# Router logits from the turned x and the scanned states in four column strips

## What is computed

```python
# attention part: x is (2, 2048, 256)
decays = sigmoid(x @ Wd + bd);  inj = x @ Wi + bi
states = scan(h -> d * h + i)                      # along the 2048 tokens
attn = layernorm(states) * gamma + beta + x
x = layernorm(x + attn)                            # called y below
# routed feed-forward part, E = 8 experts, 4 chosen per token
gate = y @ Wg.T + routing_bias
weights = softmax over the 4 largest of gate
out = swiglu(y, shared) + sum_e weights_e * swiglu(y, expert_e)
x = layernorm(y + out)
```

## Time and profile before

| | |
|---|---|
| median of 3 runs | 996.76 us (995.49 to 996.99) |
| the profiled execution's own time | 993.37 us |
| its span | 991.6 us |
| PE busy | 972.4 us, 98% |
| DVE busy | 559.6 us, 56% |
| ACT busy | 508.9 us, 51% |
| POOL busy | 544.6 us, 55% |

### The profile page before, as it was taken

How to read it: one execution, slowest core, us unless ns; L and a number is a source line. 1 busy time by engine, 2 the same in 40 slices (tenths; PEclk the granted TensorE clock), 3 DMA queues, 4 the chain that set the end, 5 groups by cost and what they waited for, 6 DMA issues and landing times.

```text
span 991.6 us, 25401 instructions
## 1 busy us (share of the span) xinstructions
PE 972.4 (98%) x8054; PEld 799.8 (81%) x8054; DVE 559.6 (56%) x1411; ACT 508.9 (51%) x1250; POOL 544.6 (55%) x513
## 2 busy tenths in 40 slices
PE   9998999999999999999999999999999999999997
PEld 4665666788887888888788878788888887887886
DVE  4998687745544455545444545454455454544686
ACT  3676354455554555555444545445455554554366
POOL 4554027766733347623955016076888880885873
PEclk9999999999999999999999999999999999999999
DMA  6959024355542333353245214228764882795785
GB/s 229 248 139 184 1 55 131 94 161 146 166 114 78 104 92 97 98 173 95 61 144 145 49 48 128 54 50 190 127 98 75 127 124 53 109 131 87 101 146 144
DMA packets 168051, 113.86 MB, mean 115 GB/s; under 512 B 113596, under 2 KB 160191, under 8 KB 166848
## 3 DMA queue, kind: packets, MB, share of 16 engines
q0 software_dynamic: 29808, 58.37, 27.5%
q1 hardware_dynamic: 115888, 33.15, 16.4%
q10 hardware_dynamic: 22304, 21.76, 6.6%
HBM read 47.09 MB, written 43.12 MB: 91 GB/s over the span
## 4 chain that ended last, share of the span: by engine, by line
PE 83%; POOL 6%; DVE 4%; DMA 3%; issue 3%; ACT 1%; SPq 1%; POOLq 0%; ACTq 0%; DVEq 0%
PE psA L1072 51%; PE psB L1103 21%; PE psA L1020 5%; POOL y_sum L758 3%; DMA rows_by_place<-y_rows,place 2%; POOL rows_by_place L694 2%; PE psB L1106 1%; PE psC L1054 1%; PE psA L1103 1%; DMA y_sum<-rows_by_place,place 1%; PE psB L1033 1%; PE psC L1047 1%; PE psC L1174 0%; SPq L518 0%; DVE g_lo L1504 0%
## 5 line engine op out<-in xcount | busy, mean ns | idle before, releaser
L873 ACT ACTIVATE sil<-psA 128x256 f32<-128x256 f32 (+1 forms) x456 | 178.8, 399 | 283.6 <-PE psA L1072 259.1
L758 POOL DMA_INDIRECT y_sum<-rows_by_place,place x128 | 199.7, 1560 | 82.8 <-issue 38.0
L1494 DVE SCALAR_TENSOR_TENSOR g<-psA,sil 128x256 f32<-128x256 f32 (+1 forms) x160 | 72.0, 450 | 306.5 <-ACT sil L873 306.3
L1072 PE MATMUL psA<-xb_odd,work 128*128 128x256 f16 x1980 | 221.1, 273 | 0.5 <-issue 0.5
L1072 PEld LDWEIGHTS psA<-xb_odd,work 128*128 128x128 f16 x1980 | 193.2, 98 | 24.1 <-issue 1.5
L1103 PE MATMUL psB<-work,g_hi 128*128 128x256 f16 x1260 | 211.1, 273 | 0.0
L1072 PE MATMUL psA<-xb,work 128*128 128x256 f16 x1782 | 199.0, 273 | 2.2 <-issue 1.1
L1072 PEld LDWEIGHTS psA<-xb,work 128*128 128x128 f16 x1782 | 173.8, 98 | 23.9 <-issue 3.8
L1494 DVE SCALAR_TENSOR_TENSOR psC<-psA,sil 128x256 f32<-128x256 f32 (+3 forms) x296 | 133.1, 450 | 77.6 <-ACT sil L873 71.2
L1103 PE MATMUL psB<-work,g_lo 128*128 128x256 f16 x630 | 171.7, 273 | 0.0
L705 POOL DMA_INDIRECT rows_by_place<-y_rows,place x96 | 95.2, 992 | 135.1 <-DMA rows_by_place<-y_rows,place 121.3
(11 more groups left out here) (176 smaller groups left out, 1033.3 us busy)
## 6 DMA issues: line engine op xcount, KB each, us to landing
stage<-wpack POOLq DMA_DIRECT2D x9, 2176.0 KB, 8.9
rows_by_place<-eb ACTq DMA_DIRECT2D x57, 256.0 KB
work<-xT SPq DMA_DIRECT2D x7, 512.0 KB, 6.0
work<-half_beta SPq DMA_DIRECT2D x6, 512.0 KB, 4.8
work<-x_tok POOLq DMA_DIRECT2D x6, 512.0 KB, 6.5
rows_by_place<-eb ACTq DMA_DIRECT2D x6, 384.0 KB
rows_by_place<-zeros SPq DMA_DIRECT2D x1, 2112.0 KB, 13.2
rows_by_place<-y_rows,place POOLq DMA_INDIRECT x128, 2.5
```

The costliest lines, as they stand in the source:

```text
L758: pool.indirect_dma_start(out=y_sum[:, n, :], out_offset=None, in_=xs, in_offset=bass.IndirectOffsetOnAxis(ap=place[:, k, n:n + 1], axis=0 ...
L873: act.activation(sil[r0:r0 + n, c % SLOTS, 0:T], psA[0:n, chunk_bank(c, T), 0:T], ACT.Silu, scale=1.0 / (XS * WS)).then_inc(silu_ready, 1)
L1072: last = pe.matmul(dst, W[:, ws, k, ci, :], xb[slot][:, KD * xs_ + k, 0:T], start=(k == 0 and n == 0), stop=(k == KD - 1 and n == 2))
L1494: dve.scalar_tensor_tensor(gated_rows(g, c, 0, n, T), src, 1.0 / (XS * WS), sil[r0:r0 + n, c % SLOTS, 0:T], ALU.mult, ALU.mult).then_inc(g ...
```

## The change

The normalized row is y = rs2 * (rs1 * (state - mean) * gamma + x + beta/2 - mean2), where rs2 carries a factor two in the kernel's scaling, so the logits are linear in x and in the states up to the factors rs1 and rs2 of a token. The gate weights are centred once (their column means subtracted), both plain, for x, and multiplied by gamma and centred again, for the states. TensorE multiplies xt and st, which lie turned in SBUF already, with these weights: the weights are stationary, 32 columns wide (8 plus 8 of use, the rest zero), and each of the four token tiles of a step writes its own 32 partitions of PSUM (Q * j), in float32. ScalarE copies the sums and adds the part of beta as a bias, TensorE turns them with one transpose, ScalarE copies them once more, and POOL combines the two parts with rs1, rs2 and the routing bias in four operations.

- gone: y_turned, turned, gates, VectorE's logits, the BRIDGE matmuls, tile yT
- new at the start: weight_sums and beta_sum (TensorE), centre_first and centre_second (VectorE, ahead of the scans), two memsets of POOL, one small copy of ScalarE
- new per step: gate_sums, turn_parts, copy_sums, copy_parts, POOL's logits
- xT has three buffers, the one of yT being the third; a load waits for gate_sums of the step three before it, and the first fetch for the third load instead of the first
- psC is used by the new sums; rstd1 and first_norm wait for the logits of two steps before
- in step 6 the first up chunk stands ahead of gate_sums(7); chunks 1 and 2 follow the loop

```diff
+            def logits(s):
+                b, g0 = s % B, tok(s) // P
+                scaled, summed, normed_ = (gate_parts[:, n, :, :] for n in range(3))
+                pool.wait_ge(parts_ready, s + 1)
+                pool.wait_ge(rstd2_ready, s + 1)
+                g = gate_tally
+                g.add(pool.tensor_tensor(scaled, parts[:, b, :, E:2 * E],
+                                         rs1[b][:, :].unsqueeze(2).to_broadcast([P, JT, E]), ALU.mult))
+                g.wait()
+                g.add(pool.tensor_tensor(summed, scaled, parts[:, b, :, 0:E], ALU.add))
+                g.wait()
+                g.add(pool.tensor_tensor(normed_, summed, rs2[b][:, :].unsqueeze(2).to_broadcast([P, JT, E]),
+                                         ALU.mult))
+                g.wait()
+                pool.tensor_tensor(gate[:, g0:g0 + JT, :], normed_, rb.unsqueeze(1).to_broadcast([P, JT, E]),
+                                   ALU.add).then_inc(logits_ready, 1)
...
                 rstd2(s)
+                logits(s)
...
-            def turned(s):
-
-                act.wait_ge(yT_turned, s + 1)
-                act.activation(yT, psC[:, :, :], ACT.Copy).then_inc(yT_ready, 1)
+            def copy_sums(s):
+                act.wait_ge(parts_summed, s + 1)
+                if s:
+                    act.wait_ge(parts_turned, s)
+                act.activation(part_rows[:, :], psC[:, 0, P * (s % B):P * (s % B + 1)], ACT.Identity,
+                               bias=beta_part[:, 0:1]).then_inc(parts_copied, 1)
+            def copy_parts(s):
+                act.wait_ge(parts_turned, s + 1)
+                if s >= B:
+                    act.wait_ge(logits_ready, s - B + 1)
+                act.activation(parts[:, s % B, :, :],
+                               psC[:, 1, P * (s % B):P * (s % B + 1)]
+                               .rearrange("p (t q) -> p t q", q=Q)[:, :, 0:2 * E], ACT.Copy).then_inc(parts_ready, 1)
...
+            def weight_sums():
+                for n in range(2):
+                    if n:
+                        pe.wait_ge(centring_steps, KD + 1)
+                    for k in range(KD):
+                        rhs = centred[:, k * E:(k + 1) * E] if n else wg[:, k * E:(k + 1) * E]
+                        last = pe.matmul(psC[:, 1, 2 * P + n * E:2 * P + (n + 1) * E], ones32[:, :], rhs,
+                                         start=(k == 0), stop=(k == KD - 1))
+                    last.then_inc(sums_ready, 1)
...
+            def gate_sums(s):
+                b = s % B
+                if s >= B:
+                    pe.wait_ge(parts_copied, s - B + 1)
+                for n, src in enumerate((xt[s % XT], st[b])):
+                    if n:
+                        pe.wait_ge(states_ready, 2 * s + 2)
                     for k in range(KD):
+                        for j in range(JT):
+                            last = pe.matmul(psC[Q * j:Q * (j + 1), 0, P * b:P * (b + 1)],
+                                             turned_weights[:, n, k, :], src[:, k, j * P:(j + 1) * P],
+                                             start=(n == 0 and k == 0), stop=(n == 1 and k == KD - 1))
+                last.then_inc(parts_summed, 1)
...
             products(1, [0])
             pe.wait_ge(small_loaded, 16)
             pe.wait_ge(consts_ready, NCONST)
+            weight_sums()
+            beta_sum()
+            gate_sums(0)
             states(0)
             products(1, [1])
...
-                if s:
-                    y_turned(s - 1)
+                turn_parts(s)
...
-                if s >= EARLY:
-                    up(SH, 0, [s - EARLY], TL, early_slot(0))
-                if s:
-                    gates(s - 1)
+                    up(SH, 0, [0], TL, early_slot(0))
                 if s + 1 < NSTEP:
+                    gate_sums(s + 1)
                     states(s + 1)
-            y_turned(NSTEP - 1)
-            up(SH, 0, [2], TL, early_slot(0))
-            gates(NSTEP - 1)
+            up(SH, 0, [1, 2], TL, early_slot(0))
             up(SH, 0, [3, 4, 5], TL, early_slot(0))
...
+            centre_first()
+            centre_second()
             for s, m in ((0, 0), (0, 1), (1, 0)):
                 scan(s, m)
```

More of the change, by code:

```diff
@@ L194, in build @@
         eb = sb("eb", [P, JL, D], F32)
+        ones32, part_rows = (eb[:, 0, n * P:(n + 1) * P] for n in range(2))
+        parts = eb[:, 1, 0:B * JT * 2 * E].rearrange("p (b t e) -> p b t e", b=B, t=JT)
+        gate_parts = eb[:, 2, 0:3 * JT * E].rearrange("p (n t e) -> p n t e", n=3, t=JT)
+        centred = eb[:, 2, 3 * JT * E:(3 * JT + KD) * E]
         row_weights = ([sb(f"row_weights{n}", [P, JB, E], F32) for n in range(2)]
@@ L209, in build @@
         passed = sem("passed")
-        xT_loaded = [sem(f"xT_loaded{b}") for b in range(B)]
+        xT_loaded = [sem(f"xT_loaded{b}") for b in range(B + 1)]
         x_loaded = [sem(f"x_loaded{b}") for b in range(B)]
@@ L846, in shared_high @@
                     .then_inc(shared_high_ready, 1)
-            for s in range(AHEAD):
-                acts(s)
+            acts(0)
+            acts(1)
+            act.wait_ge(beta_summed, 1)
+            act.activation(beta_part[:, 0:1], psC[:, 1, 3 * P:3 * P + 1], ACT.Copy).then_inc(beta_part_ready, 1)
+            act.wait_ge(beta_part_ready, 1)
+            copy_sums(0)
             for s in steps:
@@ L1045, in y_turned, with beta_sum @@
+            def beta_sum():
+                pe.wait_ge(turned_weights_ready, 1)
                 for k in range(KD):
                     for j in range(JT):
[L1047 to L1052, removed]
-                    for k in range(KD):
-                        last = pe.matmul(psC[:, 0, j * E:(j + 1) * E], yT[:, k, j * P:(j + 1) * P],
-                                         wg[:, k * E:(k + 1) * E], start=(k == 0), stop=(k == KD - 1))
-                last.then_inc(logits_summed, 1)
+                        last = pe.matmul(psC[Q * j:Q * (j + 1), 1, 3 * P:3 * P + 1], turned_weights[:, 0, k, :],
+                                         half_beta_cols[:, k:k + 1], start=(k == 0), stop=(k == KD - 1))
+                last.then_inc(beta_summed, 1)
@@ L1325, in shared_low, with centre_first, centre_second @@
                         dve.tensor_copy(lo[r:end, full:m], hi[r:end, full:m]).then_inc(shared_low_ready, 1)
-            def logits(s):
-                g0 = tok(s) // P
-                dve.wait_ge(logits_summed, s + 1)
-                dve.tensor_tensor(gate[:, g0:g0 + JT, :], psC[:, 0, 0:JT * E].rearrange("p (t e) -> p t e", e=E),
-                                  rb.unsqueeze(1).to_broadcast([P, JT, E]), ALU.add).then_inc(logits_ready, 1)
+            def centre_first():
+                dve.wait_ge(sums_ready, 1)
+                for k in range(KD):
+                    c.add(dve.scalar_tensor_tensor(turned_weights[:, 0, k, 0:E], psC[:, 1, 2 * P:2 * P + E], -1.0 / D,
+                                                   wg[:, k * E:(k + 1) * E], ALU.mult, ALU.add))
+                c.wait()
+                for k in range(KD):
+                    ins = dve.tensor_scalar(centred[:, k * E:(k + 1) * E], turned_weights[:, 0, k, 0:E],
+                                            gamma_cols[:, k:k + 1], None, ALU.mult)
+                c.add(ins)
+            def centre_second():
+                dve.wait_ge(sums_ready, 2)
+                c.wait()
+                dve.tensor_single_scalar(half_beta_cols[:, :], beta_cols, 0.5, ALU.mult)
+                for k in range(KD):
+                    ins = dve.scalar_tensor_tensor(turned_weights[:, 1, k, E:2 * E], psC[:, 1, 2 * P + E:2 * P + 2 * E],
+                                                   -1.0 / D, centred[:, k * E:(k + 1) * E], ALU.mult, ALU.add)
+                ins.then_inc(turned_weights_ready, 1)
+            c = Tally(dve, centring_steps)
             ngroup, turns, nblock, upto, b_upto, start, limit, tail = (cnt[:, n, :] for n in range(8))
@@ L1585, in _ @@
             ffn_block(0, TL, beside=routed_beside(0))
-            logits(NSTEP - 1)
             t.wait()
```

72 lines of the change are left out of this document (44 added, 28 removed).

## The result

The median is 1000.68 us (998.91 to 1001.95, 5 runs) against 995.49 (994.08 to 996.99, 5 runs) for the kernel before beside it: 1.0055 times, 95% interval 1.0041 to 1.0068, so slower, by about half a per cent. The profiled execution of after took 1001.72 us, its span is 1000.0.

The account below looks back on a forecast made before the run. TensorE, busy 98%, was taken as the bound, so only the opening before it resumes at 116.81 us could matter. Terms of +7.05, +0.2, +1.1 and -3.9 gave +4.45 on the 996.76 median: 1001.2 us, own range 999 to 1004, stated 995.5 to 1009.5.

Parts of the forecast that it names:

- The start: Opening, up to T(1): VectorE's scans queue behind the centring, first scan at 18.55 instead of 9.99; +7.05 us, the largest term.
- T(1): End of step 1's second moments on VectorE; forecast at 41.8 us instead of 34.73.
- The strips: TensorE's gate_sums per step: four strips writing disjoint partitions should overlap, 1.3 us taken, between 0.85 and 3.4.
- G: Time of TensorE's gate_sums matmuls per step, taken as 1.3 us; the sum hardly reacts up to 2.2.
- The loop: T(1) to T(6): POOL's added logits delay rstd1's power, which holds VectorE's scan; 51.95 against 51.77, +0.2 us.
- The last step: T(6) to T(7): logits(6) stands ahead of rstd1(7) and the second fetch; 8.85 instead of 7.73, +1.1 us.
- Behind the loop: From X to TensorE's resumption behind routing: third and fourth chunks run during chosen_early; -3.9 us (3.6 to 4.2).
- X: T(7), the end of step 7's second moments on VectorE; 94.23 us before, 102.6 predicted.
- The sum: All terms at TensorE's resumption behind the routing decision: 7.05 + 0.2 + 1.1 - 3.9 = +4.45 us, 121.3 instead of 116.81.
- Rivals 1: Loop: POOL never holds VectorE's scan, so -4.2 instead of +0.2; total +0.05, 996.8 us; chance 0.18.
- 3 (VectorE alone): VectorE alone sets the pace everywhere behind step 1; total -4.8, 992 us; chance 0.10.
- Rival 2: TensorE's strips run one after another, its step taking 11.3 us; total +12, 1008.8 us; chance 0.17.

Follow-up runs that it names:

- the scans first: Changed kernel with VectorE's scans of step 0 each put ahead of one half of the centring; 0.9999 times the kernel before.
- the kernel with fillers: Changed kernel plus matmuls of zeros with unread results in TensorE's idle stretches (7, 28 and 24); 1.0056 times the kernel before.
- one strip: Changed kernel plus 16 more matmuls like gate_sums per step from step 1, all into one strip of 32 partitions, result unread; 1.0237 times the kernel before.
- both edits: Changed kernel with scans ahead of centring and POOL's logits(s - 1) ahead of rstd2(s); 0.9935 and, in another set, 0.9966 times the kernel before.
- the logits late: Changed kernel with POOL's logits(s - 1) moved ahead of rstd2(s), after rstd1(s) and add_x(s + 1); 0.9992 times the kernel before.

## Why the prediction came out as it did

- **The start** (+7.05 at T(1), measured +8.80). Right in place and cause: with the scans first 4.6 of it go. Its size was short by 1.75. The scan came 0.36 later than 18.55; the rest, 1.4, is TensorE's clock, which the prediction thought about only behind the loop, and which the kernel with fillers gives back (1.38). TensorE waits 0.84, 0.40 and 1.59 us within the four microseconds of the centring; then the second half of gate_sums takes 1.08 and states(0) 1.97 instead of 1.04. The weight fetch was issued at 26.70, as forecast (27), and cost nothing.
- **The strips** (G 1.3 between 0.85 and 3.4). Measured 1.01, by the control against one strip 3.4. The lower end was nearer, for the reason given: nothing orders one strip behind another. By the Trainium skill (TensorE: Matmul & The Clock Gate, Part 3, Packing small matmuls), G would be an estimated 1.4 from three strips of 512 columns; four strips of 128 columns in float32 do better here.
- **The loop** (+0.2, measured +1.30: 53.07 against 51.77). The right pair of engines and nearly the right price, but the wrong one waits. The prediction had the scan wait 0.95 for POOL's power. In fact the scan is first by 0.07 and POOL's rstd1 is held behind it, and then the product with rs1 waits 1.18 (0.90 in the steps with low_rows) instead of 0.95 and 0.77. Three times 0.23 and twice 0.13 are 0.95 of the 1.1 us that were missing. The Trainium skill (SBUF — State Buffer, on the shared port pair) has the rule that whichever starts first holds it for the whole instruction: the 1.19 at 59.52 agrees, and the rule cuts both ways. POOL's four operations took 0.24 and 0.25 each, 1.3 with their gaps, not 1.1.
- **The last step** (8.85, measured 9.05). Right, against 7.73 before: rstd1(7) comes late behind logits(6) and the second fetch, and the product waits 1.60 instead of 0.24. With both edits it is gone (7.74); the 8.85 with the logits late alone is TensorE's clock.
- **Behind the loop** (-3.9, measured -4.13). The cause named, the third chunk at X + 0.5 instead of X + 5.0, fits: with the chunk held back again 3.7 are gone, though part of that is the clock. The lower clock of the chunks (5.76 for the two instead of 4.06) costs nothing at the resumption; the prediction paid 0.3. The limit that is left is ScalarE's normed(7) ahead of the third silu, which the prediction had in its sum (third gated at X + 6.7, measured X + 6.05).
- **The sum.** At the resumption it gave +4.45, measured +7.29: 2.8 short (start 1.75, loop 1.1, last step 0.2, less 0.2 in the tail). The time of 1000.68 nevertheless meets the 1001.2, and that is partly luck. The forecast stood on the 996.76 of three runs, while before ran at 995.49 beside the changed kernel, so as a difference +4.45 was forecast and +5.19 measured. Of the +7.29 at the resumption only 5.19 are seen in the medians: the two spans differ by 8.4, but before's profiled execution lies 2.1 below the median beside it and after's 1.0 above. The prediction's lift of 3.4 assumed that such a gap carries over to the changed kernel; nothing of it was seen, and it more than made up for the 2.8 that the sum was short. So the verdict was right for its reasons, the four mechanisms with the start as the largest; that the number was is in part errors that cancel. Whether the quick microseconds of before's profiled execution lie ahead of its resumption or behind it was not measured.
- Rivals 1 (scan never held) and 3 (VectorE alone) would need a loop of 47.6: it exists, but only with the logits moved (47.86). By the prediction's own terms a plain step of VectorE needs 9.0, not 9.1 (10.36 less 0.81, 0.30 and 0.24); with the logits moved the plain steps take 8.96 to 9.22. Rival 2 (no overlap) is ruled out by the 1.01, and the one-strip kernel shows what 3.4 us more a step would have cost: X 12.8 later.

## What to carry to other kernels

A change that takes 1.45 us a step off the busiest engine (1.69 + 0.88 gone, 1.01 + 0.11 new) gave nothing, because the work went to the engine that shares a dependence loop with the next busiest: look for the idle gap of the receiving engine and put the moved work there, not between two links of the chain; that place alone was worth 5.2 us here. New preparation belongs behind the first instructions of the recurrent chain, not ahead of them (4.6 us, of which about 1.4 are TensorE's clock, lost in the waits of that preparation). And before adding a gap between a profiled execution and the median to a sum, ask in which stretch it lies.

## What the hardware showed that I had not expected

- A POOL operation on 128x4 numbers, 0.20 us when alone, takes 1.19 when it starts 0.07 behind a VectorE scan of 1.27; the power, 1.01, took up to 2.01.
- Gaps of 0.84, 0.40 and 1.59 us between TensorE's work were followed by half clock (8 transposes 1.97 instead of 1.09), and how long it lasts differs between executions of one kernel (7.08 or 8.66 for the next 16 records, 7.03 at full clock).
- Filler matmuls kept the granted clock at 1.00 and shortened the stretch they were meant for, yet in no kernel did they make the time shorter; with them both edits went from 0.9966 to 1.0000. Why is open.
